# Transposed one-hots of the attention stage by a comparison of two tensors, the partition number read from PSUM

## What is computed

```python
h = (x @ W).reshape(n, H, C)                      # H = 4 heads of C = 64
al_src = jnp.einsum('nhc,hc->nh', h, a_src)
al_dst = jnp.einsum('nhc,hc->nh', h, a_dst)
e = jax.nn.leaky_relu(al_src[src] + al_dst[dst], 0.2)
emax = jax.ops.segment_max(e, dst, num_segments=n)
ee = jnp.exp(e - emax[dst])
denom = jax.ops.segment_sum(ee, dst, num_segments=n)
alpha = ee / (denom[dst] + 1e-16)
out = jax.ops.segment_sum(h[src] * alpha[:, :, None], dst, num_segments=n)
```

## Time and profile before

| | us |
|---|---|
| median of the runs | 5138.23 |
| lowest, highest | 5134.06, 5144.11 |
| profiled execution | 5136.53 |
| its span, first to last instruction | 5134.7 |
| the attention stage's gathers in it | 2397.1 to 4565.1 |

### The profile page before, as it was taken

The page is one execution under the profiler, slowest core; times in us unless marked ns, Lnnn a source line. Parts: engine busy times, 40 slices in busy tenths (PEclk is TensorE's granted clock), DMA queues, the critical chain, the costliest instruction groups (busy, mean ns, idle before and its releaser), DMA issues. The chain is left out here.

```text
span 5134.7 us, 76750 instructions
## 1 busy us (share of the span) xinstructions
PE 3748.7 (73%) x19865; PEld 2834.2 (55%) x19865; DVE 3239.1 (63%) x9212; ACT 2421.9 (47%) x7596; POOL 3470.0 (68%) x3620
## 2 busy tenths in 40 slices
PE   6277777777777777775667667676777677668998
PEld 4156666666666666564555555454555555545665
DVE  6655555555555555553777777777777777774454
ACT  5323333333333333333666766666766766661221
POOL 4377777777777777774777777777777777742222
PEclk9589999999999999998777777777777777778999
DMA  4656666665665566663455555555555555534221
GB/s 132 204 162 171 170 170 170 170 170 170 170 171 168 168 170 170 170 170 97 138 148 153 148 149 152 147 150 151 151 144 152 148 152 150 148 107 146 75 78 48
DMA packets 338812, 767.24 MB, mean 149 GB/s; under 512 B 79990, under 2 KB 178392, under 8 KB 338238
## 3 DMA queue, kind: packets, MB, share of 16 engines
q0 software_dynamic: 202704, 594.02, 42.2%
q1 hardware_dynamic: 135662, 168.07, 10.0%
HBM read 712.95 MB, written 58.60 MB: 150 GB/s over the span
## 5 line engine op out<-in xcount | busy, mean ns | idle before, releaser
L826 POOL DMA_INDIRECT flow_rows<-table,edges x1708 | 1624.7, 951 | 608.9 <-issue 498.1
L1430 POOL DMA_INDIRECT gat_steps_rows<-table,edges x1712 | 1646.9, 962 | 557.0 <-issue 485.6
L1862 PE MATMUL gat_steps_sum_ps<-gat_steps_rows,gat_steps_onehot 128*128 128x264 f32 x3424 | 1116.1, 481 | 271.1 <-DVE acc L1583 259.1
L1173 PE MATMUL flow_sum_ps<-flow_rows,flow_onehot 128*128 128x256 bf16 x5124 | 779.0, 294 | 412.4 <-DMA flow_rows<-table,edges 319.8
L1862 PEld LDWEIGHTS gat_steps_sum_ps<-gat_steps_rows,gat_steps_onehot 128*128 128x128 f32 x3424 | 761.9, 234 | 479.9 <-DVE acc L1583 303.6
L1173 PEld LDWEIGHTS flow_sum_ps<-flow_rows,flow_onehot 128*128 128x128 bf16 x5124 | 504.8, 105 | 612.7 <-issue 282.2
L1729 ACT ACTIVATE gat_steps_rows<-gat_steps_rows 128x64 f32<-128x64 f32 x3424 | 828.5, 334 | 0.0
L899 DVE TENSOR_TENSOR acc<-flow_sum_ps,acc 128x256 f32 x854 | 359.8, 421 | 660.1 <-PE flow_sum_ps L1173 640.4
L1583 DVE TENSOR_TENSOR acc<-gat_steps_sum_ps,acc 128x264 f32 x856 | 370.5, 433 | 241.0 <-PE gat_steps_sum_ps L1862 165.8
L1225 PE MATMUL flow_y_ps<-flow_w,flow_hid 128*128 128x256 f32 x1568 | 438.5, 405 | 83.4 <-DVE flow_x_blk L985 44.7
L1215 PE MATMUL flow_hid_ps<-flow_xn_t,flow_w 128*128 128x128 f32 x3136 | 459.8, 295 | 8.7 <-ACT flow_hid L1108 8.7
(11 more groups left out here) (381 smaller groups left out, 5438.3 us busy)
## 6 DMA issues: line engine op xcount, KB each, us to landing
gat_steps_drow<-drow SPq DMA_DIRECT2D x107, 512.0 KB
gat_steps_rows<-table,edges POOLq DMA_INDIRECT x1712
flow_rows<-table,edges POOLq DMA_INDIRECT x1708
expert_w<-in_L_ffn_w SPq DMA_DIRECT2D x16, 1024.0 KB, 7.4
table<-start_parts SPq DMA_DIRECT2D x49, 192.0 KB, 1.8
gat_steps_mask<-masks SPq DMA_DIRECT2D x428, 12.1 KB
table<-flow_row SPq DMA_DIRECT2D x49, 130.0 KB, 2.7
gat_steps_self_row<-table SPq DMA_DIRECT2D x49, 130.0 KB
```

Source lines behind the costliest of these rows:

```text
L826: nc.gpsimd.indirect_dma_start(out=rows[n % RING][:, t, :], out_offset=None, in_=g["table0"][:, :], in_offset=bass.IndirectOffsetOnAxis(ap ...
L1173: ins = t.matmul(sum_ps[i % 2][:, :], onehot[i // AHEAD % 2][:, i % AHEAD * T + u, :], rows[i % RING][:, u, part * D:(part + 1) * D], star ...
L1430: nc.gpsimd.indirect_dma_start(out=rows[w % RING][:, t, 0:RW], out_offset=None, in_=g["table1"][:, :], in_offset=bass.IndirectOffsetOnAxis ...
L1862: ins = t.matmul(sum_ps[(w * SPW + s) % BANKS][:, :], onehot[k][:, i, :], rows[r][:, i, :], start=(i == s * T), stop=(i == s * T + T - 1))
```

## The change

`onehot_t` is built by a comparison of two tensors: the first operand is `drow` as before, the second one column of PSUM, repeated along the row. `iota_ps` grows by that column, which is filled by one more copy at the start of the stage. The other use of `iota_ps` names its first 128 columns.

```diff
-        iota_ps = ps("iota_ps", P)
+        iota_ps = ps("iota_ps", P + 1)
...
-                v.tensor_scalar(onehot_t[:, :], drow[k][:, :], g["pidx"][:, 0:1], None, ALU.is_equal).then_inc(onehot_t_ready, 1)
+                v.tensor_tensor(onehot_t[:, :], drow[k][:, :], iota_ps[:, P:P + 1].broadcast_to([P, W * P]), ALU.is_equal
+                                ).then_inc(onehot_t_ready, 1)
...
-                v.tensor_tensor(onehot[k][:, :, :], iota_ps[:, :].unsqueeze(1).broadcast_to([P, W, P]), dst,
+                v.tensor_tensor(onehot[k][:, :, :], iota_ps[:, 0:P].unsqueeze(1).broadcast_to([P, W, P]), dst,
...
-            v.tensor_copy(iota_ps[:, :], g["iota"][:, :])
+            v.tensor_copy(iota_ps[:, 0:P], g["iota"][:, :])
+            v.tensor_copy(iota_ps[:, P:P + 1], g["pidx"][:, :])
```

## The result

| | us |
|---|---|
| changed kernel, median of 20 runs | 5130.32 (5119.2 to 5138.45) |
| kernel before, median of 20 runs beside them | 5139.1 (5134.06 to 5148.08) |
| ratio, 95% interval | 0.9977 [0.9971, 0.9983] |
| profiled execution of the changed kernel, its span | 5135.09, 5133.3 |

The change makes the kernel 0.23% faster, 0.17 to 0.29%. Forecast was 0.26%. The net is right; its two terms are not: the gain was larger than I said and the cost was not hidden. The profiled execution is the second longest of its 20, so I read durations and waits from it and not the difference of the spans (1.4 us).

What follows compares the result with a forecast made beforehand. POOL's unbroken gather queue was taken to set the attention stage's pace. -14.2 us of stretch + 1 us for later loads = -13.2 on 5136.5: 5123.3; with the runs' median 1.7 us higher, 5125.0 us, range 5116 to 5144.

Steps and rivals of the forecast that it cites:

- its two terms: Attention stage: -14.2 us from POOL's gathers no longer stretched, +1 us once at the stage's end for later drow loads.
- POOL is the pace, and the stretch goes: Attention stage: POOL's gathers run without pause, 20.26 us a window; their stretch beside L1489, 14.2 us, goes.
- The one gather that the prediction held against the inference on descriptor making: A 1.06 us gather beside `edges`, against the inference that descriptor making doesn't need SBUF's read side; no change to the sum.
- The comparison takes 2.27 us: VectorE's L1489: the new instruction takes 2.27 us for 0.79, so 1.48 us more work a window.
- It is hidden: VectorE's slot: the added 1.48 us fits into 1.85 us of room before the scan, leaving about 0.25 us a window.
- The replay: Windows 4 to 106 stepped through with measured slot lengths: 19.86 us against POOL's 20.13, last scan 13.9 us earlier.
- The sum had 1 us there: Stage's end: 1 us counted once, for drow loads issued later that can push rows back.
- A: The forecast: POOL keeps the pace, its stretch beside L1489 goes, longer comparison hidden; 5118 to 5131 us; chance 0.53.
- C: Rival: VectorE's slot becomes the pace, slower once it grows 0.43 us more than counted; 5142 to 5155 us; chance 0.16.
- B: Rival: no change, as POOL stays stretched or half the gain is lost to later drow loads; 5130 to 5141 us; 0.31.

Runs made afterwards that it cites:

- e3: Changed kernel plus four wasted f32 128x128 products on TensorE ahead of its wait for onehot_t: 6492.58 us, 1.0265 of the kernel before, under the experiments' conditions.
- f4: Same edit as e3 (changed kernel, four wasted TensorE products ahead of the onehot_t wait), run again: 6483.07 us, 1.0273 of the kernel before.
- h2: Changed kernel with only TensorE's dst_terms products moved behind the second quarter of sums, comparison left ahead of the scan: 6076.09 us, 0.9642 of the kernel before.
- f1: The changed kernel unaltered, as control under the experiments' conditions: 6422.04 us, 1.016 of the kernel before.
- f3: Same edit as e4 (changed kernel, partition number as 128 bf16 columns in PSUM), run again: 6345.09 us, 1.0043 of the kernel before.
- e2: Changed kernel with the old tensor_scalar back and a wasted 1312-column tensor_tensor ahead of it: 6429.5 us, 1.0169 of the kernel before.
- e4: Changed kernel with the partition number as 128 bf16 columns in PSUM, repeated over the tiles, for the comparison: 6342.27 us, 1.0031 of the kernel before.

## Why the prediction was right, and where it was not

**POOL is the pace, and the stretch goes: right, and mis-sized.** 265 gathers overlap the new L1489; their mean is 0.945 us and none is above 0.96, where 82 of 151 were above 0.97, the longest took 1.44 and the mean was 1.041. 120 lie wholly inside it, mean 0.945, as the 122 inside L1535 (0.946) had promised. These are taken from the traces in ns; the prediction's 1.042, 0.948, 121 and 104 come from rows rounded to 10 ns, and no sum changes by it. The rule of the Trainium skill, "SBUF — State Buffer", section "Who interferes with whom", that an instruction with one SBUF input leaves GpSimd alone agrees in all 265. Mis-sized was the rest, which I called not edited: the gathers stretched beside other lines fell from 107 to 81, and their excess from 13.5 to 8.9 us. The slot has shifted against POOL's queue, and they overlap the short operations of `edges` less often (82 overlaps with the two `gat_steps_z` operations before, 42 after). 14.2 + 4.6 is 18.8 us, and 19.1 was measured. The one gather that the prediction held against the inference on descriptor making doesn't decide: it also overlaps a `tensor_scalar` (L1561, at 3308.23). But 65 of the 107, with 8.4 of the 13.5 us, overlap none, and these do speak against it.

**The comparison takes 2.27 us: right.** 2.288 us. The idle time ahead of it stayed, 52.0 us in place of 51.0.

**It is hidden: wrong.** This is the step that failed. The replay said 19.86 us a window against POOL's 20.13. Between the scans of windows 4 and 106, 102 windows apart, the changed kernel needs 20.23 us, and POOL 20.09. So the slot falls behind by 0.14 us a window, 14 us in all, less the first windows in which there was room; the lag rose by 11.5. The sum had 1 us there. Of the missing 0.37 us, 0.33 lies between a scan and the next L1489, which I had taken as fixed at 17.57 and which is 17.90. It is VectorE's wait at its additions: 200.6 us for sums in place of the 165.8 of this row of the kernel before, with the third and fourth addition idle before them for 0.63 and 0.64 us in place of 0.51 and 0.53. The growth is in the 47 slots that begin a block's normalisation (18.17 to 19.34 us), while the other 55 became shorter (17.05 to 16.67).

```profile
DVE acc L1583 <- PE gat_steps_sum_ps L1862: 165.8, 294, 1.4
```

One such slot in both traces, TensorE's sums of the second quarter first, then VectorE's third and fourth addition. The kernel before:

```profile
3157.88 2.05 PE L1862 MATMUL gat_steps_sum_ps<-gat_steps_rows,gat_steps_onehot 128*128 128x264 f32 x8
```

```profile
3159.17 0.43 DVE L1583 TENSOR_TENSOR acc<-gat_steps_sum_ps,acc 128x264 f32 x1 [0.45 <-PE gat_steps_sum_ps L1862]
3160.06 0.43 DVE L1583 TENSOR_TENSOR acc<-gat_steps_sum_ps,acc 128x264 f32 x1 [0.46 <-PE gat_steps_sum_ps L1862]
```

The changed kernel:

```profile
3157.65 3.75 PE L1864 MATMUL gat_steps_sum_ps<-gat_steps_rows,gat_steps_onehot 128*128 128x264 f32 x8
```

```profile
3159.91 0.43 DVE L1584 TENSOR_TENSOR acc<-gat_steps_sum_ps,acc 128x264 f32 x1 [1.42 <-PE gat_steps_sum_ps L1864]
3161.53 0.43 DVE L1584 TENSOR_TENSOR acc<-gat_steps_sum_ps,acc 128x264 f32 x1 [1.19 <-PE gat_steps_sum_ps L1864]
```

The same eight products take 3.75 us in place of 2.05. The rows by microsecond (PE busy, count, PEclk, DMA share, GB/s) show the granted clock, first before and then after:

```profile
3156.00:3157.00 1.00, 1.00 (x4) 0.66 0.36 100
3157.00:3158.00 1.00, 1.00 (x11) 1.00 0.39 108
...
3160.00:3161.00 1.00, 1.00 (x6) 1.00 0.62 133
```

```profile
3157.00:3158.00 1.00, 1.00 (x6) 0.50 0.30 83
...
3160.00:3161.00 1.00, 1.00 (x4) 0.50 0.60 143
3161.00:3162.00 1.00, 1.00 (x5) 0.94 0.52 114
```

Both had TensorE at the lower level, 1.2 GHz, when the sums began (at 3153.89 and 3152.70). Before, 2.4 GHz was back at 3156.7; after, at 3161.1, behind the sums that VectorE waits for. Ahead of it TensorE had idled once, 2.83 us for the scores, and then 0.43; after, 1.37 us for the scores and 1.59 for `onehot_t`. The other slots agree. The means over windows 4 to 105 of both traces, for the second quarter's sums (the lengths of the eight products are added up, overlaps and all):

| before to after | 47 slots that begin a normalisation | other 55 |
|---|---|---|
| granted clock over these sums | 0.91 to 0.70 | 0.86 to 0.93 |
| 2.4 GHz back, after the first sum's start, us | 4.5 to 6.7 | 4.9 to 4.2 |
| eight products, us | 3.53 to 4.45 | 3.60 to 3.42 |
| VectorE's waits for sums in the slot, us | 1.92 to 3.03 | 1.19 to 0.83 |
| from the scan to the next L1489, us | 18.17 to 19.34 | 17.05 to 16.67 |

Of the 1.16 us by which the first kind grew 1.11 are waits for sums, and of the 0.38 by which the other shrank 0.37. In both kinds the waits go with the clock, and the whole stage's products of these sums are busy 1149.9 us in place of 1116.1. That TensorE's clock sets the slot's growth is thus read from 102 slots of two traces. e3 and f4 show that what TensorE does at `onehot_t` moves this clock, but under other conditions and without a gain in time; that the longer comparison moved it here is argued and not shown.

**The rivals.** A has the time, but its picture is C's: the slot is the pace from window 33 on, with ScalarE waiting for rows in 18 windows, under the 20 that I had set as C's mark, and the last scan late. C's third mark, POOL waiting for sums, did not come (0.3 us at most). VectorE's wait before the scan is 36.4 us, below the 50 to 90 that A has. C came with 0.37 us where I had said that 0.43 makes it slower than before, and the larger gain on POOL's side covered it. B's stretch under the new instruction did not come. The replay as such holds: with 0.37 us added, an instruction of 2.64 on its scale, it gives back some 10 of its 13.9 us (an estimate between its 2.5 and 2.7), and the lag rose by 11.5. Its input of 17.57 was wrong. So the forecast's 0.26% was met with luck, by two errors of opposite sign, 5 us too little gain and 10 us too little cost, and by the 4 us between the traced execution and the ratio.

**What I should have weighed.** I gave 0.25 us of room in 20 as "thin, but it holds". The replay moved every wait inside the slot rigidly with VectorE; the waits on TensorE are not rigid. Nor did I price the second wait that the edit lengthens, TensorE's at `onehot_t_ready`, with `ends` and the sums queued behind it: I named the delay and gave it no time. h2 shows what the products' place there can cost, though only under the conditions of the experiments.

## What to carry to other kernels

An instruction that holds up another engine can be exchanged for a slower one that doesn't, but the exchange pays in full only while the slot with the slower one stays shorter than the other engine's queue; count the room in that slot before and after, and treat a few per cent of it as none. Where an in-order queue waits for a tile whose products are needed late, try moving these products down the queue: where the exchange alone lost 1.6%, exchange and move together gained 3.6% (f1, h2); at 5139 us this was not run. And a comparison of 16-bit data with a step-1 16-bit operand in PSUM gave both, no hold on POOL (none of f3's 144 gathers beside it took over 0.95 us) and 1.22 us in place of 2.29.

## What the runs showed of the hardware that I had not expected

- The same program took 5139 us in one measurement and 6309 to 6324 us on three chips in the experiments. There ScalarE's fade went on 2 to 11 us after TensorE's last record (94 places in f1, 798 us of waiting), and a change that is 0.23% faster at 5139 us is 1.6% slower.
- A bf16 comparison of two tensors, one of them bf16 in PSUM with step 1, ran 2048 columns in 1.221 us; with one f32 column of PSUM repeated it took 2.288 us.
- A gather stretched by the `tensor_scalar` took up to 1.44 us in the kernel before (the one that starts at 4059.8; the earlier trace rows shows one of 1.30), and up to 1.47 us in e2, in place of 0.95.
- With the comparison at 2.29 us in place of 0.79, eight products of TensorE's sums took 4.45 us in place of 3.53 in the slots that begin a normalisation, at a granted clock of 0.70 in place of 0.91.
- Not tried: h2 or e4's comparison under the conditions in which the kernel before takes 5139 us. Whether they beat the change there is open; POOL's 20.09 us a window leave at most some 11 us to win.
